# Zeros over the exponentials of later keys, in place of mask products, in six cross-attention units

## The reference

```python
q = relu(query @ Wq + bq); k = relu(key @ Wk + bk); v = relu(value @ Wv + bv)
scores = einsum('bhqd,bhkd->bhqk', q, k) / sqrt(16)
causal = tril(ones((256, 256), bool))
scores = where(causal, scores, -2.0**32 + 1)
out = einsum('bhqk,bhkd->bqhd', softmax(scores), v) + q
return layer_norm(out, gamma, beta)
```

## Time and profile before

| | before |
|---|---|
| time, median of three runs | 625.91 us (622.7 to 629.24) |
| profiled execution, time | 624.59 us |
| profiled execution, span from first to last instruction | 622.8 us |
| TensorE busy | 520.7 us, 84% |
| VectorE busy | 338.3 us, 54% |
| ScalarE busy | 218.9 us, 35% |
| GpSimd busy | 146.8 us, 24% |
| mean granted clock of TensorE | 0.941 of 2.4 GHz |
| mask products on TensorE under transposed cross scores | 96, 30.2 us busy with overlaps |

### The profile page before, as it was taken

The page is one execution under the profiler, slowest core; times in us unless marked ns, Lnnn a source line. Parts: engine busy times, 40 slices in busy tenths (PEclk is TensorE's granted clock), DMA queues, the critical chain, the costliest instruction groups (busy, mean ns, idle before and its releaser), DMA issues. The chain is left out here.

```text
span 622.8 us, 12856 instructions
## 1 busy us (share of the span) xinstructions
PE 520.7 (84%) x5092; PEld 404.9 (65%) x5092; DVE 338.3 (54%) x952; ACT 218.9 (35%) x491; POOL 146.8 (24%) x160
## 2 busy tenths in 40 slices
PE   5179487959989989989999879799798999999960
PEld 4047265737666667767767656477587888888850
DVE  3547343746677877877677967684263202232114
ACT  2004125234445544544554625453521111232103
POOL 4000003002103004004104166000123755132330
PEclk9669779989999999999999989799999999999995
DMA  2999935693595585585449556345666634888214
GB/s 87 118 145 140 161 62 87 116 106 43 78 136 97 76 132 99 85 120 101 96 54 157 79 109 189 52 162 196 224 233 228 202 52 76 247 300 244 23 20 137
DMA packets 58840, 78.97 MB, mean 127 GB/s; under 512 B 9454, under 2 KB 52077, under 8 KB 55708
## 3 DMA queue, kind: packets, MB, share of 16 engines
q1 hardware_dynamic: 42236, 39.57, 41.1%
q10 hardware_dynamic: 10400, 33.29, 16.9%
q0 software_dynamic: 6144, 5.29, 5.3%
HBM read 40.32 MB, written 13.74 MB: 87 GB/s over the span
## 5 line engine op out<-in xcount | busy, mean ns | idle before, releaser
L956 DVE TENSOR_REDUCE negm<-nat 128x4 f32<-128x512 f32 (+2 forms) x192 | 120.0, 641 | 88.7 <-PE nat L532 86.5
L769 ACT ACTIVATE probs<-byk 128x512 f32<-128x512 f32 (+1 forms) x192 | 105.8, 562 | 116.0 <-PE byk L532 114.3
L532 PE MATMUL nat<-arena 96*128 96x128 bf16 (+2 forms) x512 | 73.8, 248 | 0.0
L532 PE MATMUL byk<-arena 99*128 99x128 bf16 (+2 forms) x512 | 71.8, 242 | 0.0
L532 PEld LDWEIGHTS nat<-arena 96*128 96x128 bf16 x512 | 46.9, 102 | 16.3 <-issue 3.2
L532 PEld LDWEIGHTS byk<-arena 99*128 99x128 bf16 x512 | 45.7, 99 | 18.1 <-issue 1.1
L1212 POOL TENSOR_TENSOR resk<-fk,parts_k 128x512 f32<-128x512 f32 x8 | 9.3, 1158 | 182.3 <-ACT fk L708 125.8
L528 PE MATMUL nat<-window_q,identb 128*128 128x384 bf16 (+1 forms) x96 | 35.9, 374 | 18.8 <-DMA arena<-parts_k 13.7
L528 PE MATMUL byk<-window_k,identb 128*128 128x384 bf16 (+1 forms) x96 | 34.2, 356 | 18.1 <-DMA arena<-mT 17.7
L670 PE MATMUL work<-yn_T,arena 128*128 128x160 f32 x256 | 40.1, 305 | 2.4 <-DVE r_s L1123 2.4
L670 PE MATMUL work<-woT,arena 128*128 128x160 f32 x256 | 39.8, 304 | 0.0
(11 more groups left out here) (189 smaller groups left out, 895.3 us busy)
## 6 DMA issues: line engine op xcount, KB each, us to landing
arena<-parts_q SPq DMA_DIRECT2D x96, 128.0 KB, 5.1
arena<-parts_k SPq DMA_DIRECT2D x96, 128.0 KB, 5.4
arena<-in_ffn_wi ACTq DMA_DIRECT2D x12, 1024.0 KB, 5.5
arena<-in_ffn_wo ACTq DMA_DIRECT2D x12, 1024.0 KB, 8.4
expert_x<-ranked ACTq DMA_DIRECT2D x4, 650.0 KB, 4.9
v_s<-expert_x SPq DMA_DIRECT2D x20, 130.0 KB
xres<-in_x ACTq DMA_DIRECT2D x8, 256.0 KB, 5.5
token_y<-xres SPq DMA_DIRECT2D x8, 256.0 KB, 5.0
```

The costliest lines, as they stand in the source:

```text
L532: last = nc.tensor.matmul(bank[:, i * w:(i + 1) * w], lhsT, rhs, start=False, stop=(i == heads - 1), skip_group_check=True)
L769: nc.scalar.activation(dst, src, ACT.Exp, scale=0.25).then_inc(exp_ready, 1)
L956: V.tensor_reduce(dst, src, AX, ALU.max, negate=True).then_inc(nat_free[job % 2], 1)
```

## The change

In the cross units of `ZEROED` (4, 6, 8, 10, 12 and 13) the T jobs run without mask product, each score product opening its own columns. The exponentials then hold numbers for later keys too. After the second T job of a group GpSimd writes zeros over the later keys in the first block of `probs` (Z0), after the third job in the second block (Z1), by an affine select on 128x4x128 elements in place. Each adds one to `zeroed`, and PV of these units waits for `zeroed` instead of the exponential. PV's slot moves from 22.2 to 22.9. Units 14 and 15 and the self-attention keep their mask products, and so do the natural scores.

```diff
+ZEROED = [UNIT_OF["c", b] for b in range(6)]
...
         for g in range(G):
-            add(n0 + 22.2 - sooner + 3 * g if k < last - 1 else t_slot(k, 3 * g + 2) + (1.1 if g < G - 1 else 0.5), "PV", k, g)
+            if k in ZEROED:
+                add(n0 + 20.1 + 3 * g, "Z0", k, g)
+                add(n0 + 21.3 + 3 * g, "Z1", k, g)
+            add(n0 + (22.9 if k in ZEROED else 22.2) - sooner + 3 * g if k < last - 1 else t_slot(k, 3 * g + 2) + (1.1 if g < G - 1 else 0.5), "PV", k, g)
...
+            def bare_scores(bank, heads, w, emit_pair):
+
+                for i in range(heads):
+                    lhsT, rhs = emit_pair(i)
+                    last = nc.tensor.matmul(bank[:, i * w:(i + 1) * w], lhsT, rhs, start=True, stop=True, skip_group_check=True)
                 return last
...
-                if i < 2:
+                if k in ZEROED:
+                    if i < 2:
+                        h0 = 4 * g + 2 * i
+                        last = bare_scores(bank, 2, T, lambda h: (ks[0:KR + MR, h0 + h, 0:P], q[0:KR + MR, h0 + h, 0:T]))
+                    else:
+                        h0 = 4 * g
+                        last = bare_scores(bank, 4, P, lambda h: (ks[0:KR + MR, h0 + h, P:T], q[0:KR + MR, h0 + h, P:T]))
+                elif i < 2:
...
             def PV(k, g, layer, b):
-                pe.wait_ge(exp_ready, JOBS * k + 3 * g + 3)
+                if k in ZEROED:
+                    pe.wait_ge(zeroed, 2 * (G * ZEROED.index(k) + g + 1))
+                else:
+                    pe.wait_ge(exp_ready, JOBS * k + 3 * g + 3)
...
+            def later_keys(at, k, g):
+
+                kept = probs[:, g % 2, :, at:at + P]
+                g_.affine_select(out=kept, in_=kept, compare_op=ALU.is_ge, fill=0.0, base=0, pattern=[[0, 4], [1, P]],
+                                 channel_multiplier=-1).then_inc(zeroed, 1)
+
+            def Z0(k, g, layer, b):
+                pool.wait_ge(exp_ready, JOBS * k + 3 * g + 2)
+                later_keys(0, k, g)
+
+            def Z1(k, g, layer, b):
+                pool.wait_ge(exp_ready, JOBS * k + 3 * g + 3)
+                later_keys(T, k, g)
```

More of the change, by code:

```diff
@@ L317, in attention_and_experts @@
         byk_full = sems("byk_full", 2); exp_ready = sem("exp_ready")
-        pv_full = sem("pv_full"); yT_ready = sem("yT_ready")
+        pv_full = sem("pv_full"); zeroed = sem("zeroed"); yT_ready = sem("yT_ready")
         part0 = {side: sem(f"part0_{side}") for side in "qk"}
@@ L533, in bank_scores @@
                 return last
+            def bare_scores(bank, heads, w, emit_pair):
+                for i in range(heads):
+                    lhsT, rhs = emit_pair(i)
+                    last = nc.tensor.matmul(bank[:, i * w:(i + 1) * w], lhsT, rhs, start=True, stop=True, skip_group_check=True)
+                return last
             def N(k, j, layer, b):
@@ L1267, in ES @@
                                         in_=ye[x % 2][:, 1, 0:ZW], in_offset=None, compute_op=ALU.add).then_inc(y_stored[x % 2], 16)
-            walk({"CK": CK, "XB": XB, "XA": XA, "VC": VC, "GS": GS, "ES": ES})
+            walk({"Z0": Z0, "Z1": Z1, "CK": CK, "XB": XB, "XA": XA, "VC": VC, "GS": GS, "ES": ES})
 def by_partition(a):
```

## The result

The changed kernel took 662.04 us (median of four runs, 657.49 to 666.85) against 624.77 us for the kernel before, run on the same chip between them (622.7 to 629.24). The ratio is 1.0587, with a 95% interval from 1.0545 to 1.0628. The direction was the forecast one, but 37.3 us came where 18.1 were predicted (644 against 625.91), and 662 lies outside the range of 634 to 654.

A forecast was written before the change was run, and what follows sets the result against it. TensorE was taken to set the pace, VectorE close behind. Stops 16.5 + third groups 0.3 + clock 7.0 + units 12 and 13 1.5 - saving 6.7 = 18.6 us more, 644 us for a median; range 634 to 654.

The forecast's parts named there:

- The stops: Fourth groups of units 4, 6, 8, 10: PV waits for the select behind CK, 3.9 + 3 x 4.2 = 16.5 us.
- The small losses of 0.3 us at third groups: First four units: hand-overs and a select need 0.84 us; the tightest place, unit 10's third group, has 0.82; 0.3 us lost.
- The clock behind the stops: After each of four stops TensorE runs at 1.2 GHz for a while, losing 1.75 us each, 7.0 us in all.
- The saving: Mask products removed from TensorE in six units: at most 10.6 us, of which 6.7 us was expected to be won.
- I keep three quarters, 0.75 x 4 x 1.76 = 5.3 us: Units 4, 6, 8, 10: removed mask time partly falls ahead of waits for VectorE, so 5.3 us is won.
- The lock: VectorE and GpSimd share an exclusive port pair; the change adds 48 holders, at the very worst 31 us of VectorE.
- The second rival: Selects hinder VectorE or take longer than the prologue's: 3.4 + 2.6 us more, 650 us; chance 0.12.
- part of the rest is off the path: VectorE during selects: most time is row maxima at full speed, part of the rest off the path, against the 31 us.
- Units 12 and 13: Selects behind the scatter's issues on GpSimd make unit 12's products late: 1.5 us taken, between nothing and 4 us.
- They run into the 4.46 us: Unit 12's last two products, 1 and 3 us later still, run into TensorE's 4.46 us wait for unit 15's queries.
- The clock stays up: First rival: same stops, but the clock stays up and stops swallow some later waits: 637 us; chance 0.16.
- The third: Rival: stops and saving cancel, full 10.6 us won, clock stays, unit 12 covered: 630 us, within 1%; chance 0.06.

The follow-up runs named there:

- e1: The changed kernel with CK later on GpSimd, so the last select of units 4, 6, 8 and 10 stands ahead of it: 635.2 us, ratio 1.0128.
- e5: The changed kernel with units 12 and 13 left as before and the last select ahead of CK in units 4 to 10: 629.96 us, ratio 1.0075.
- e6: The changed kernel with 36 extra TensorE products ahead of the fourth product with v in units 4, 6, 8 and 10: 655.65 us, ratio 1.0489.
- e2: The kernel before without the mask products in the six units and no selects in their place: 624.14 us, ratio 0.995.
- e3: The changed kernel with the mask products kept beside the selects: 662.04 us, ratio 1.0586.
- e8: e1 with the same 48 selects over 4 columns of each block in place of 128: 624.54 us, ratio 0.9987.

## Why the prediction was wrong, point by point

The 37.3 us come apart by medians: 16.4 the four stops, 10.4 what hung on them (after less e1, less the stops), 5.2 units 12 and 13 (e1 less e5), 5.3 the rest of units 4 to 10 (e5 less before). The runs of before beside these kernels lie between 624.65 and 625.79, so each part is known to a few us only.

**The stops: right.** 16.5 us predicted, 16.4 measured, at the four places named, and a select of 0.65 us against 0.64. So close a select is partly luck, since its price was drawn out to 512 columns from bf16 rows of 128 and 192; the stop, mostly KC, fk and CK, hardly hangs on it. The small losses of 0.3 us at third groups did not show in units 4 to 10.

**The clock behind the stops: right in kind, too small.** The prediction took 1.75 us for each stop, from 3.49 us at half clock in the earlier trace rows. In after the half clock lasted 3.41 to 6.13 us behind a stop and cost 1.6 to 2.8, 9.0 us in all: from PV to the 80th product behind it TensorE took 9.1 to 10.3 us, in before 7.5. With the half clock of the middle of the units, 10.4 us hung on the stops by the medians, where 7.0 were put down; e6 takes back 6.4 of them by keeping TensorE busy. The other 4.0 lie within the spread of the executions, and the traces below name no cause beside the clock.

**The saving: a step that failed.** "I keep three quarters, 0.75 x 4 x 1.76 = 5.3 us" rested on the earlier trace rows, where the waits for VectorE were 5.5 us in 13 pieces, as if these were all that could take the saving up. They grow with it: e2, with nothing added, waits 2.4 us longer in units 4 to 10 and is 1.6 to 3 us faster for all six units; e3, with nothing removed, is as slow as after. The earlier trace rows said it already, with VectorE busy 32.84 us of 40 and each unit giving the natural scores their banks back only as fast as VectorE takes the maxima: an engine at 82% that TensorE waits for 13 times is a bound in places, whatever the average.

**The lock: named and priced at nothing in the sum.** The second rival had the mechanism, with 31 us of selects as its worst case, and then was priced by a longer select instead. The select was not longer, and VectorE was held up all the same, on the path. The prediction's reason, that "part of the rest is off the path", is what failed: the short operations held up stand ahead of row maxima in VectorE's list. Saving and lock together are the largest error of the sum, 10.3 of 18.7 us: they make e5's 5.3 us loss out of a forecast 5.0 us gain. The traces show how these come about. The rows go from the start of unit 4 to the end of unit 11, with the columns of the earlier trace rows, in before, e2, e1, e8, e5 and after:

```profile
167.91:349.64 181.73, 168.57 (x1592) 124.75 (x1590) 139.32 (x350) 90.11 (x206) 33.05 (x28) 1.00 0.67 102
168.52:348.40 179.88, 163.38 (x1543) 121.14 (x1541) 138.70 (x350) 89.36 (x207) 33.03 (x28) 0.99 0.69 103
168.35:351.67 183.32, 163.55 (x1543) 120.56 (x1541) 141.58 (x350) 89.47 (x206) 53.67 (x60) 0.99 0.68 101
167.35:347.66 180.31, 163.53 (x1543) 121.12 (x1541) 138.11 (x350) 89.47 (x206) 40.20 (x60) 0.99 0.69 102
166.85:353.22 186.37, 166.50 (x1543) 123.04 (x1541) 141.66 (x350) 89.70 (x206) 53.34 (x60) 0.97 0.67 99
169.22:382.26 213.04, 177.32 (x1543) 129.87 (x1541) 142.85 (x350) 90.46 (x206) 53.51 (x60) 0.91 0.56 87
```

The removal itself was sized rightly. A T job of two heads and one of four take 0.33 and 0.45 us on TensorE, from start to what follows, in before, and 0.22 and 0.23 in e2, and TensorE's busy time is 5.2 us shorter in e2, although 3.0 us of it are at half clock, which costs some 1.5. But its idle time, the length less the busy time, grows from 13.2 to 16.5 us, and 1.8 of the 7.0 us are left. In e1 the idle time is 19.8 us and 1.6 us are lost; in e8, which differs only in the length of the selects, it is 16.8. So in these units the selects' length costs 3.0 us in these traces, nearly all in waits for VectorE. e5 waits as e1 does (19.9 us idle), but TensorE is busy at half clock for 9.8 us where e1 has 3.4, and it loses 4.6 us. After takes 29.7 us longer than e1, 15.9 of them idle and 13.8 busy with the same 1543 products: it has 32.9 us at half clock.

**Units 12 and 13: wrong in size.** "They run into the 4.46 us": they did, and 3.9 us of it went. But the stops were 8.2 us long in all and were followed by half-clock stretches: 4.1 to 7.2 us in place of 0.1 net (1.5 of loss less 1.4 of saving). The prediction counted the issues well, 1.6, 1 and 3 us for what was 1.52, 1.48 and 4.38, and left the clock out here, although its own had a stretch at 0.50 behind just that wait.

**The rivals.** "The clock stays up" (637) is ruled out by the half clock behind each of the four stops. The third (630) needed the full saving and no half clock, and had neither. "It pays" (620) fell too, and e2 shows that it had no ground: even with the selects free the gain is 1.6 to 3 us. The sum's three errors all pointed one way, and the range was too narrow for them, since it took in a select that is long but not one that is in the way. No version that was run is faster than before with the keys masked; e8 without most of the masking only equals it.

## What to carry to other kernels

When work moves to an idle engine, read its list for what it will stand behind (one select behind CK cost 26.8 of 37.3 us), and then read what the other engines do during it: here a select of 0.65 us on GpSimd was paid for by small operations of VectorE, although GpSimd was idle for most of the time. Before counting work taken off the busiest engine as time, look at the engine it already waits for in places; an experiment that only removes, as e2, gives the ceiling at once (0.5%). And count an idle gap of TensorE with the clock behind it: here 4.1 us of stop cost 5.6 to 6.9.

## What the runs showed of the hardware

Operations of VectorE on 256 numbers took 0.56 to 0.62 us beside a select of 0.65 us, three times their 0.17 to 0.18.

Behind stops of TensorE of 4.1 us the granted clock was 0.50 for 3.4 to 6.1 us; with products running in the stops it stayed at 1.00.

The same program ran in 625.4 and 639.3 us with nearly the same waits and a mean granted clock of 0.947 and 0.923. Idle gaps of about 2 us were followed by 1.2 GHz in some executions and by 2.4 GHz in others. A difference of a few us between two single traces of such a kernel is therefore no evidence by itself.
